# Relative attention: one of four max subtractions from VectorE to GpSimd, the output bias from GpSimd to TensorE

## The reference

```
q, k, val = heads(x @ Wq + bq), heads(x @ Wk + bk), heads(x @ Wv + bv)     # 16 heads of 8
pos = sinusoid(S, D) @ Wp + bp
content_score = einsum('bhsp,bhtp->bhst', q + u, k)
pos_score = relative_shift(einsum('bhsp,htp->bhst', q + v, pos))
weights = softmax((content_score + pos_score) / sqrt(8), axis=-1)
out = einsum('bhst,bhtp->bhsp', weights, val)                              # heads side by side
x = x + out @ Wo + bo
```

## Time and profile before

| | |
|---|---|
| median of 3 runs | 1391.49 us (1387.2 to 1395.02) |
| the profiled execution | 1387.54 us, its span 1385.7 us |
| mean granted TensorE clock | 0.953 |
| busy over the span | PE 1139.1 us, DVE 990.6, ACT 835.2, POOL 562.5 |
| subtraction of the maxima, VectorE L1370 | 128 times, 96.0 us in all |
| bias addition, GpSimd L929 | 32 times |

### The profile page before, as it was taken

How to read it: one execution, slowest core, us unless ns; L and a number is a source line. 1 busy time by engine, 2 the same in 40 slices (tenths; PEclk the granted TensorE clock), 3 DMA queues, 4 the chain that set the end, 5 groups by cost and what they waited for, 6 DMA issues and landing times. The chain is left out here.

```text
span 1385.7 us, 40959 instructions
## 1 busy us (share of the span) xinstructions
PE 1139.1 (82%) x12567; PEld 744.3 (54%) x12567; DVE 990.6 (71%) x3667; ACT 835.2 (60%) x1653; POOL 562.5 (41%) x750
## 2 busy tenths in 40 slices
PE   2788887887598888898589878888888758999998
PEld 1344444454355555555378456666666544665665
DVE  2588888885366666666466369999998739887885
ACT  1487878786277777777423378888887432342331
POOL 4777777772222222222010146666665911111120
PEclk9899999999599999999889999999999778999999
DMA  8000000000100000000022078888887540000000
GB/s 220 9 2 1 0 0 0 0 2 2 56 8 2 1 0 0 0 0 0 17 60 61 14 214 237 236 232 232 234 234 210 155 130 1 8 16 9 8 8 16
DMA packets 170484, 91.33 MB, mean 66 GB/s; under 512 B 8922, under 2 KB 168804, under 8 KB 170132
## 3 DMA queue, kind: packets, MB, share of 16 engines
q1 hardware_dynamic: 169860, 88.05, 23.3%
q0 software_dynamic: 528, 2.10, 0.5%
HBM read 52.11 MB, written 38.01 MB: 65 GB/s over the span
## 5 line engine op out<-in xcount | busy, mean ns | idle before, releaser
L821 POOL TENSOR_TENSOR rr<-ms_eps,minus_half 128x16 f32<-128x16 f32 x64 | 185.2, 2912 | 11.6 <-DVE ms_eps L1029 11.6
L550 PE MATMUL psum<-identb,stacks 128*128 128x128 bf16 x1800 | 138.3, 224 | 34.9 <-DVE stacks L1078 13.5
L1163 DVE TENSOR_REDUCE rowmax<-psum 128x4 f32<-128x768 f32 x128 | 123.1, 961 | 60.8 <-PE psum L2130 60.8
L550 PEld LDWEIGHTS psum<-identb,stacks 128*128 128x128 bf16 x1800 | 111.5, 100 | 65.7 <-issue 24.8
L1364 DVE CUSTOM_DVE_ANT_0 summed<-psum,pos_score 128x128 f32<-128x128 f32 x512 | 117.9, 285 | 23.5 <-PE psum L2330 19.9
L1930 ACT ACTIVATE pos_rows<-psum 128x512 f32<-128x512 f32 x72 | 43.0, 597 | 144.0 <-PE psum L2514 137.1
L2372 PE MATMUL psum<-consts,summed 128*128 128x128 f32 x512 | 84.4, 289 | 43.1 <-DVE summed L1370 41.7
L1068 DVE TENSOR_REDUCE rowmax<-psum 128x4 f32<-128x512 f32 x128 | 84.9, 686 | 34.6 <-PE psum L1996 34.6
L1816 ACT ACTIVATE probsT<-psum 128x512 f32<-128x512 f32 x128 | 76.9, 601 | 54.0 <-PE psum L641 39.8
L641 PE MATMUL psum<-probsT,values 128*32 128x128 f32 x2048 | 85.2, 282 | 26.1 <-DVE attn L667 21.7
L882 POOL TENSOR_TENSOR rest<-staged,stacks 128x128 f32<-128x128 f32 x32 | 13.7, 428 | 220.4 <-ACT stacks L533 220.4
(11 more groups left out here) (320 smaller groups left out, 3065.1 us busy)
## 6 DMA issues: line engine op xcount, KB each, us to landing
skew<-pos_rows SPq DMA_DIRECT2D x128, 258.0 KB, 3.8
pos_score<-skew SPq DMA_DIRECT2D x128, 256.0 KB, 4.0
X<-in_x_dram POOLq DMA_DIRECT2D x1, 2048.0 KB, 12.1
ctxT<-in_ctx_dram SPq DMA_DIRECT2D x1, 2048.0 KB, 10.6
yT<-in_ctx_dram SPq DMA_DIRECT2D x32, 64.0 KB, 1.8
ctxT<-in_ctx_dram SPq DMA_DIRECT2D x32, 64.0 KB, 1.8
out_dram<-X SPq DMA_DIRECT2D x8, 256.0 KB, 2.3
pos_rows<-in_ctx_dram SPq DMA_DIRECT2D x25, 64.0 KB, 1.9
```

What stands on the lines that cost most here:

```text
L550: last = pe.transpose(turned[:, t, :], stacks[:, which, 2 * t:2 * t + 2, :].rearrange("s h k -> s (h k)"), identb[:, :])
L821: pool.tensor_tensor(out=rr[:, par, i * H:(i + 1) * H], in0=ms_eps[:, i * H:(i + 1) * H], in1=minus_half[:, 0:H], op=ALU.pow).then_inc(A.r ...
L1163: dve.tensor_reduce(rowmax[:, par, PT * r:PT * r + PT].rearrange("s (h b) -> s b h", b=2), B.max_space, AX.X, ALU.max, negate=True).then_i ...
```

## The change

VectorE no longer subtracts the maxima of round 3, except in the last two batches; GpSimd does it, between `ln_rstd` and the split of K, and counts it on a semaphore of its own, `less_last`. `P.less` counts the other three rounds (`subtracted`). TensorE's `turn_less` of round 3 and VectorE's `add_max` of the next round 1 wait for `less_last`. GpSimd no longer adds the output bias. The bias becomes a fourth set of three bf16 rows in `qkvo_parts`, made by VectorE with the other three during the recurrence, and `output` begins with a product of ones and these rows.

```diff
-        bias3_top = sb("bias3_top", [3, 3, D], BF16)
-        bias3_rest = sb("bias3_rest", [3, 3, D])
+        bias3_top = sb("bias3_top", [3, 4, D], BF16)
+        bias3_rest = sb("bias3_rest", [3, 4, D])
...
-        qkv_parts = sb("qkv_parts", [128, 3, D], BF16)
+        qkvo_parts = sb("qkvo_parts", [128, 4, D], BF16)
...
+        def subtracted(n, r):
+
+            return n * (R - 1) + r + 1
...
-        def output(pe, q, n, weights):
+        def output(pe, q, n, weights, bias=None):
             wait(pe, q.aT, n + 1)
             wait(pe, q.x, n)
-            pe.matmul(q.y_space, attnT[:, :], weights, start=True, stop=True).then_inc(q.y, 1)
+            if bias is not None:
+                pe.matmul(q.y_space, ones3[:, :], bias, start=True, stop=False)
+            pe.matmul(q.y_space, attnT[:, :], weights, start=(bias is None), stop=True).then_inc(q.y, 1)
...
-                def output_bias(n):
-                    wait(pool, P.xn, P.base + n + 1)
-                    pool.tensor_tensor(out=X[:, at(n), :], in0=X[:, at(n), :], in1=bias_rows[:, 6:7, :], op=ALU.add)\
-                        .then_inc(P.bias, 1)
-
...
+                def take_last_max(n):
+                    wait(pool, P.add, (n + 1) * R)
+                    pool.sem_inc(k0.carry, 1)
+                    last = (R - 1) % 2
+                    pool.tensor_tensor(out=summed[:, last, :, :], in0=summed[:, last, :, :],
+                                       in1=topmost[:, last, :].unsqueeze(2).broadcast_to([S, PT, S]), op=ALU.subtract).then_inc(P.less_last, 1)
+
                 def body(b, par, left):
                     if left >= 3:
                         split(b + 3, Q)
                     if left >= 4:
                         ln_rstd(pool, P, b + 4)
+                    if left >= 2:
+                        take_last_max(b)
                     if left >= 3:
                         split(b + 3, K)
-                    if left >= 4:
-                        output_bias(b + 4)
...
+                dve.tensor_copy(bias3_top[:, 3:4, :], bias_rows[0:3, 6:7, :]).then_inc(P.parts, 1)
                 cell(NB - 4)
...
+                dve.scalar_tensor_tensor(out=bias3_rest[:, 3:4, :], in0=bias3_top[:, 3:4, :], scalar=part_marks[:, 0:1], in1=bias_rows[0:3, 6:7, :],
                                          op0=ALU.mult, op1=ALU.add).then_inc(P.parts, 1)
...
-                    wait(dve, P.less, n * R + r - 1)
+                    wait(dve, [P.less, P.less_last][r == 1], n if r == 1 else subtracted(n, r - 2) if r > 1 else subtracted(n - 1, 2))
...
-                    take_max(b, 3)
+                    if left < 2:
+                        take_max(b, 3, P.less_last)
...
                 def turn_less(n, r):
-                    wait(pe, P.less, n * R + r + 1)
+                    wait(pe, [P.less, P.less_last][r == R - 1], n + 1 if r == R - 1 else subtracted(n, r))
                     wait(pe, P.p, n * R + r - 1)
...
-                        output(pe, P, b - 1, w_o1[:, :])
+                        output(pe, P, b - 1, w_o1[:, :], qkvo_parts[:, 3, :])
...
-                pe.wait_ge(P.parts, 6)
+                pe.wait_ge(P.parts, 8)
```

More of the change, by code:

```diff
@@ L311, in decoder @@
         P = Phase()
-        [P.proj, P.q, P.split, P.v, P.bias, P.qT_ps, P.qT, P.kT_ps, P.kT,
-         P.e, P.es, P.s, P.add, P.less, P.p, P.pT_ps, P.o, P.on, P.aT_ps, P.aT,
+        [P.proj, P.q, P.split, P.v, P.qT_ps, P.qT, P.kT_ps, P.kT,
+         P.e, P.es, P.s, P.add, P.less, P.less_last, P.p, P.pT_ps, P.o, P.on, P.aT_ps, P.aT,
          P.y, P.x, P.bqs, P.zeroed, P.pos, P.shift, P.padded, P.parts] = sems(
-            "d", "proj q split v bias qT_ps qT kT_ps kT e es s add less p pT_ps o "
+            "d", "proj q split v qT_ps qT kT_ps kT e es s add less less_last p pT_ps o "
             "on aT_ps aT y x bqs zeroed pos shift padded parts")
@@ L909, in cross_attention @@
                 ln_rstd(pool, B, 2)
-                pool.memset(qkv_parts[:, :, :], 0.0).then_inc(P.padded, 1)
+                pool.memset(qkvo_parts[:, :, :], 0.0).then_inc(P.padded, 1)
                 pool.memset(bias3_parts[:, :, :], 0.0).then_inc(C.padded, 1)
@@ L952, in relative_attention @@
                     ln_rstd(pool, P, n)
-                    output_bias(n)
                     if n >= 1:
@@ L958, in relative_attention @@
                 ln_rstd(pool, P, 3)
-                output_bias(3)
                 body_pairs(pool, body, tail=2)
@@ L1249, in recurrence @@
                 dve.tensor_scalar(part_marks[:, 0:1], part_marks[:, 0:1], -1.0, None, ALU.mult).then_inc(C.scaled, 1)
-                dve.tensor_copy(bias3_top[:, :, :], bias3[:, :, :]).then_inc(C.scaled, 1)
+                dve.tensor_copy(bias3_top[:, 0:3, :], bias3[:, :, :]).then_inc(C.scaled, 1)
                 dve.wait_ge(C.scaled, 9)
-                dve.scalar_tensor_tensor(out=bias3_rest[:, :, :], in0=bias3_top[:, :, :], scalar=part_marks[:, 0:1], in1=bias3[:, :, :],
+                dve.scalar_tensor_tensor(out=bias3_rest[:, 0:3, :], in0=bias3_top[:, 0:3, :], scalar=part_marks[:, 0:1], in1=bias3[:, :, :],
                                          op0=ALU.mult, op1=ALU.add).then_inc(C.scaled, 1)
                 dve.wait_ge(C.scaled, 10)
-                dve.tensor_copy(bias3_top[:, :, :], bias3_rest[:, :, :]).then_inc(C.scaled, 1)
+                dve.tensor_copy(bias3_top[:, 0:3, :], bias3_rest[:, 0:3, :]).then_inc(C.scaled, 1)
                 dve.wait_ge(C.scaled, 11)
                 dve.wait_ge(C.padded, 1)
-                dve.scalar_tensor_tensor(out=bias3_parts[0:3, :, :], in0=bias3_top[:, :, :], scalar=part_marks[:, 1:2], in1=bias3_rest[:, :, :],
+                dve.scalar_tensor_tensor(out=bias3_parts[0:3, :, :], in0=bias3_top[:, 0:3, :], scalar=part_marks[:, 1:2], in1=bias3_rest[:, 0:3, :],
                                          op0=ALU.mult, op1=ALU.add).then_inc(C.scaled, 1)
@@ L1310, in recurrence @@
                 dve.tensor_copy(bias3_top[:, 1:3, :], bias_rows[0:3, 3:5, :]).then_inc(P.parts, 1)
+                dve.tensor_copy(bias3_top[:, 3:4, :], bias_rows[0:3, 6:7, :]).then_inc(P.parts, 1)
                 cell(NB - 4)
-                dve.wait_ge(P.parts, 2)
+                dve.wait_ge(P.parts, 3)
                 dve.scalar_tensor_tensor(out=bias3_rest[:, 0:1, :], in0=bias3_top[:, 0:1, :], scalar=part_marks[:, 0:1], in1=bias_q[0:3, 0:1, :],
@@ L1315, in recurrence @@
                 dve.scalar_tensor_tensor(out=bias3_rest[:, 1:3, :], in0=bias3_top[:, 1:3, :], scalar=part_marks[:, 0:1], in1=bias_rows[0:3, 3:5, :],
+                                         op0=ALU.mult, op1=ALU.add).then_inc(P.parts, 1)
+                dve.scalar_tensor_tensor(out=bias3_rest[:, 3:4, :], in0=bias3_top[:, 3:4, :], scalar=part_marks[:, 0:1], in1=bias_rows[0:3, 6:7, :],
                                          op0=ALU.mult, op1=ALU.add).then_inc(P.parts, 1)
@@ L1324, in recurrence @@
                 cell(NB - 3)
-                dve.wait_ge(P.parts, 4)
+                dve.wait_ge(P.parts, 6)
                 dve.tensor_copy(bias3_top[:, :, :], bias3_rest[:, :, :]).then_inc(P.parts, 1)
                 cell(NB - 2)
-                dve.wait_ge(P.parts, 5)
+                dve.wait_ge(P.parts, 7)
                 dve.wait_ge(P.padded, 1)
-                dve.scalar_tensor_tensor(out=qkv_parts[0:3, :, :], in0=bias3_top[:, :, :], scalar=part_marks[:, 1:2], in1=bias3_rest[:, :, :],
+                dve.scalar_tensor_tensor(out=qkvo_parts[0:3, :, :], in0=bias3_top[:, :, :], scalar=part_marks[:, 1:2], in1=bias3_rest[:, :, :],
                                          op0=ALU.mult, op1=ALU.add).then_inc(P.parts, 1)
@@ L1366, in add_max, with take_max @@
                     last.then_inc(P.add, 1)
-                def take_max(n, r):
+                def take_max(n, r, done=P.less):
                     wait(dve, P.add, n * R + r + 1)
                     dve.tensor_tensor(summed[:, r % 2, :, :], summed[:, r % 2, :, :],
-                                      topmost[:, r % 2, :].unsqueeze(2).broadcast_to([S, PT, S]), ALU.subtract).then_inc(P.less, 1)
+                                      topmost[:, r % 2, :].unsqueeze(2).broadcast_to([S, PT, S]), ALU.subtract).then_inc(done, 1)
                 def body(b, par, left):
@@ L2308, in project @@
                     wait(pe, P.xnT, P.base + n + 1)
-                    pe.matmul(P.ln_bank[:, 128:512], ones3[:, :], qkv_parts[:, :, :].rearrange("e w d -> e (w d)"), start=True, stop=False)
+                    pe.matmul(P.ln_bank[:, 128:512], ones3[:, :], qkvo_parts[:, 0:3, :].rearrange("e w d -> e (w d)"), start=True, stop=False)
                     pe.matmul(P.ln_bank[:, 128:512], xnT[:, :], wqkv[:, :, :].rearrange("e w d -> e (w d)"),
@@ L2466, in relative_attention @@
                 turn_attn(pe, P, NB - 1)
-                output(pe, P, NB - 1, w_o1[:, :])
+                output(pe, P, NB - 1, w_o1[:, :], qkvo_parts[:, 3, :])
             relative_attention()
```

## The result

The changed kernel takes 1508.61 us (median of 4 runs, 1504.62 to 1511.33) against 1390.43 before: a ratio of 1.0845, 95% interval 1.0801 to 1.0889. Slower, as forecast, and 25.6 us beyond the predicted 1483, inside the range.

What follows compares the result with a forecast made beforehand. VectorE was read as fullest, TensorE close behind; after the change a circle through TensorE, ScalarE and GpSimd sets the batch. 1387.5 + 64.7 (circle) + 30.8 (clock) = 1483.0 us, range 1445 to 1520.

Steps and rivals of the forecast that it cites:

- The circle: Relative attention: TensorE, ScalarE and GpSimd wait for each other in a loop through GpSimd's queue, which sets the batch time.
- Saved on VectorE, 0: The 0.69 us subtraction leaves VectorE just ahead of its 0.45 us wait for TensorE's scores, so nothing is saved.
- The size of the circle: Legs from one `turn_less` of round 3 to the next sum to 11.35 us against 9.04, +2.31 a batch.
- The clock: TensorE's 2.1 us wait for GpSimd lowers its granted clock, losing 1.1 us a batch in the mean, 30.8 us.
- Shut out by `take_max(b+1, 0)`: Rival, chance 0.16: VectorE's operation holds the shared SBUF pair against GpSimd's subtraction, up to 0.69 us a batch, 1502 us.
- The rest, 0: Bias addition leaving GpSimd, small VectorE operations in the recurrence, larger memset, wait for `P.parts`: 0, VectorE operations at most 1.4.
- 28 batches: Bodies 0 to 27 of the relative attention run the slower way, 64.7 us; bodies 28 and 29 add 0.
- The signs: Expected in the trace: 11 to 13 us batches, TensorE waiting for GpSimd's subtraction, clock well below 1.00, VectorE near 70%.

Runs made afterwards that it cites:

- e3: The changed kernel with GpSimd's body reordered: rstd of batch b+4, the subtraction, the split of Q, the split of K; 1398.97 us, ratio 1.0083 to the kernel before.
- e5: The changed kernel with TensorE repeating its attention transpose 13 times in bodies 0 to 27 before waiting for the subtraction; 1435.10 us, ratio 1.0339 to the kernel before.
- e4: The changed kernel with rstd of batch b+4 moved behind GpSimd's subtraction, the split of Q staying ahead; 1441.12 us, ratio 1.0386 to the kernel before.
- e1: The kernel before with only the output bias made a TensorE product, VectorE subtracting in all rounds; 1391.12 us against 1386.40, ratio 1.0033.

## Why the prediction was right, step by step

- *The circle*: right. Its legs have the order forecast, TensorE is at `turn_less(b, 3)` 1.6 to 2.8 us before the subtraction is done, and e3 takes it away by order alone.
- *Saved on VectorE, 0*: right; the wait for scores grew by what left (e3).
- *The size of the circle*: +2.31 a batch forecast, 10.63 - 9.04 = 1.59 measured with the clock held up (e5). Each of its terms was somewhat high. The subtraction takes 1.04 us alone, under the lower bound of 1.18 that I had taken from half an operation over 1024 columns: that row was not a clean price for this form, and why is not shown. The step to TensorE takes 0.05, not 0.17, which was a step from GpSimd to itself. 64.7 us forecast, 44.5 shown.
- *The clock*: the step that was mis-sized. I took 1.1 us a batch, "some batches lose nothing". All 26 lose, 7.58 - 5.22 = 2.36 us in the mean, 66 us in all instead of 30.8. What a microsecond at the lower clock loses was about right, 1 - 3.24 / 5.78 = 0.44 us; how long the clock stays low was not. The 2.6 us of the earlier trace rows were the length of the stretch that I had picked, not of the low clock. The row behind it, second below, still has 0.86, so that spell lasted 3.4 us; the first below shows that the one after the wait of 3.46 us went on to 1074 at least:

```profile
1071.00:1074.00 3.00, 3.00 (x25) 2.64 (x23) 1.63 (x9) 2.21 (x4) 0.64 (x2) 0.50 0.38 97
...
1104.00:1107.00 3.00, 3.00 (x36) 2.12 (x35) 1.03 (x5) 2.50 (x6) 2.90 (x5) 0.86 0.45 126
```

  In the kernel after, a granted clock of 0.79 means that about (1 - 0.79) / 0.5 = 0.42 of the time, 5.6 us of a batch, is at the lower level, and 5.6 x 0.44 = 2.5 us, near the 2.36. The wait came out longer than forecast, too. I had worked out 2.1 us with TensorE held up by VectorE as before. But in the mean of these batches that hold-up falls from 1.0 us to 0.36, and the wait for GpSimd is 2.5 us, up to 2.82. I costed a fall of the clock as an event of its own, and not what it does to the next wait. That this is what brings the clock down in every batch is argued from e4 and not shown.
- *Shut out by `take_max(b+1, 0)`*: I priced it at 0 and gave it as a rival with 0.69 a batch. It happens in 16 of the 26 batches, which take 1.38 to 1.58 us: 1.53 at 937.24, where `take_max` had begun at 937.17. In the mean it takes 0.29 us more than the 1.04 of the other ten, 8 us in all. In those ten VectorE is the one shut out, as here:

```profile
950.97 1.53 DVE L1379 TENSOR_TENSOR summed<-summed,topmost 128x512 f32<-128x512 f32 x1
```

  GpSimd's subtraction ran from 950.91 to 951.95, and the one on VectorE, 0.69 us alone, ended 0.55 us after that. The other way round, GpSimd's ends 0.90 us after `take_max`, of its 1.04. So nearly the whole of the second runs after the first. The Trainium skill's "SBUF — State Buffer", section "Who interferes with whom", has two such operations take a shared pair one after the other, and the trace agrees.
- *The rest, 0*: nearly. The bias part alone is 0.3% (e1).
- *28 batches*: right. They hold 113.4 us of the difference of the two traces, and 0.4 us are left for the bodies 28 to 31.
- *The signs*: the waits are where I said. Three sizes were off: the batches of 13.26 us lie above the 11 to 13, VectorE's share fell to 57% (22.84 of 40 us) and not to near 70%, and the subtraction takes 1.04 us where it is not shut out, under the 1.2 to 1.7.

So 44.5 + 66 + 8 is the 118 us of 28 x (13.26 - 9.04), against 64.7 + 30.8 = 95.5: two errors of opposite sign. That the total came nearer than the terms is luck.

## What to carry to other kernels

An operation that is moved to an idle engine is done when that engine's queue gets to it, not when its data are ready: look up what stands ahead of it, and whether that waits, however far round, for the reader of the moved result. Of several equal pieces, give away the one whose reader comes latest and whose absence shortens a wait; here that turned +8.5% into -0.9%. A wait on TensorE behind which its clock falls is to be priced by how long the clock then stays low, here 5.6 us of a batch, and together with the waits that the lower clock makes.

## What the runs showed of the hardware that I had not expected

Useless work on TensorE paid: 1.64 us of repeated transposes a batch (e5) raised the granted clock from 0.79 to 1.00 and took 2.4 us from the first leg.

On GpSimd a subtraction over 128x512 with a broadcast second input took 1.04 us (1.039 to 1.044 over the 30 of e4), while products and sums over 128x1024 took 2.36: more than twice as long for twice the columns.
